# Per-pair order of the projections: all four rotated key products first, the second output-weight product among the queries

## The reference

```
q_lat = x @ Wq_down;  kv_lat = x @ Wkv_down          # x is layer-normalised
q = [q_lat @ Wq_up , rope(q_lat @ Wq_rope)]          # 16 heads, 64 + 64 columns
k = [kv_lat @ Wk_up, rope(x @ Wk_rope)]
out = softmax(causal(q k^T * scale)) @ (kv_lat @ Wv_up)
x = x + out @ Wo
x = x + (silu(h @ up^T) * (h @ gate^T)) @ down^T     # ternary weights, h = layernorm(x)
```

## Time and profile before

| | |
|---|---|
| median of 3 runs | 1917.61 us (1916.95 to 1923.71) |
| profiled execution | 1922.49 us |
| its span | 1920.7 us |
| TensorE busy | 1849.0 us, 96% of the span |
| VectorE, ScalarE, GpSimd busy | 70%, 54%, 27% |
| mean granted TensorE clock | 0.985 of full speed |

### The profile page before, as it was taken

One profiled execution on the slowest core, in us unless ns is written; L12 is line 12 of the kernel. 1 busy time (PEld: TensorE's weight loads), 2 busy tenths in 40 slices (PEclk: granted clock), 3 DMA queues, 4 the chain that ended last, 5 costly groups with the idle time before them and its releaser, 6 DMA issues. The chain is left out here.

```text
span 1920.7 us, 30945 instructions
## 1 busy us (share of the span) xinstructions
PE 1849.0 (96%) x10898; PEld 1611.7 (84%) x10898; DVE 1337.0 (70%) x2818; ACT 1037.2 (54%) x2485; POOL 522.6 (27%) x314
## 2 busy tenths in 40 slices
PE   6899978899999999999999999999999799999998
PEld 4688866889998999999999999999999678777777
DVE  5466646688888888888888888888888633333333
ACT  2223326677777666667676666667666332322232
POOL 4456652111111154234235234234223000000000
PEclk9999988999999999999999999999999889999999
DMA  3399985332231222221221212212110160000000
GB/s 118 118 229 228 219 206 189 91 88 65 79 86 48 66 72 72 62 66 60 57 61 50 78 40 66 68 55 66 39 55 30 37 238 1 22 0 22 4 17 22
DMA packets 96625, 153.31 MB, mean 80 GB/s; under 512 B 12528, under 2 KB 46448, under 8 KB 96240
## 3 DMA queue, kind: packets, MB, share of 16 engines
q1 hardware_dynamic: 84976, 130.66, 23.1%
q10 hardware_dynamic: 11520, 20.98, 4.2%
HBM read 97.06 MB, written 54.53 MB: 79 GB/s over the span
## 5 line engine op out<-in xcount | busy, mean ns | idle before, releaser
L1121 ACT CAST turned_hi<-ps_turn 128x512 fp32r<-128x512 f32 (+1 forms) x576 | 313.6, 571 | 275.4 <-PE ps_turn L1306 271.4
L1077 ACT ACTIVATE probs<-ps_scores,bias 128x512 f32<-128x512 f32 (+3 forms) x640 | 401.9, 641 | 60.0 <-DVE bias L1165 59.7
L1204 DVE TENSOR_TENSOR turned_lo<-ps_turn,turned_hi 128x512 fp32r<-128x512 f32 (+1 forms) x576 | 374.6, 655 | 64.7 <-ACT turned_hi L1121 58.9
L1306 PE MATMUL ps_turn<-ident,probs 128*128 128x128 f32 x2176 | 302.7, 274 | 1.4 <-DVE turned_lo L1204 1.4
L1162 DVE TENSOR_REDUCE negmax<-ps_scores 128x1 f32<-128x512 f32 x384 | 261.9, 686 | 50.5 <-PE ps_scores L1265 45.6
L1306 PEld LDWEIGHTS ps_turn<-ident,probs 128*128 128x128 f32 x2176 | 257.3, 141 | 33.7 <-issue 2.2
L1007 POOL TENSOR_TENSOR q_lo<-q_raw,q_hi 128x512 fp32r<-128x512 f32 x64 | 82.8, 1294 | 687.7 <-ACT q_hi L1069 687.7
L1265 PE MATMUL ps_scores<-k_hi,q_hi 128*128 128x512 f32 (+2 forms) x576 | 233.7, 406 | 7.7 <-ACT probs L1077 7.5
L1325 PE MATMUL ps_o<-turned_hi,kv_hi 128*128 128x256 f32 x1088 | 227.7, 286 | 5.7 <-DVE o_lo L1210 5.7
L1325 PE MATMUL ps_o<-turned_lo,kv_hi 128*128 128x256 f32 x1088 | 224.4, 283 | 0.0
L1325 PE MATMUL ps_o<-turned_hi,kv_lo 128*128 128x256 f32 x1088 | 224.1, 283 | 0.0
(11 more groups left out here) (152 smaller groups left out, 3508.6 us busy)
## 6 DMA issues: line engine op xcount, KB each, us to landing
plainT<-plain_out ACTq DMA_DIRECT2D x64, 256.0 KB, 4.3
rotT<-rot_out SPq DMA_DIRECT2D x64, 256.0 KB, 4.3
all_signs<-signs SPq DMA_DIRECT2D x24, 512.0 KB, 2.8
q_raw<-plainT SPq DMA_DIRECT2D x128, 64.0 KB, 2.4
q_raw<-rotT SPq DMA_DIRECT2D x256, 32.0 KB, 2.1
signs<-in_W_up SPq DMA_DIRECT2D x16, 512.0 KB, 3.6
signs<-in_W_gate SPq DMA_DIRECT2D x16, 512.0 KB, 3.7
signs<-in_W_down SPq DMA_DIRECT2D x16, 512.0 KB, 3.6
```

The lines of the kernel that those rows point to most:

```text
L1077: nc.scalar.activation(probs_of(n, i)[:, h, first_key:first_key + keys], ps_scores[:, pieces.number[args] % RING, 0:keys], ACT.Exp, scale= ...
L1121: nc.scalar.copy(turned[0][:, at, cols(*args)], ps_turn[:, bank, cols(*args)]).then_inc(turned_hi_ready, 1)
L1204: nc.vector.tensor_tensor(turned[1][:, at, cols(*args)], ps_turn[:, bank, cols(*args)], turned[0][:, at, cols(*args)].bitcast(F32), ALU.su ...
L1306: last = nc.tensor.transpose(ps_turn[:, bank, (2 * b + h) * P:(2 * b + h + 1) * P], probs_of(n, i)[:, h, key:key + P], ident[:])
```

## The change

In `usual_order()` the four rotated key products come first, as in `last_order()`; the first head's output-weight product stays behind the second key product, both parts of its weights are split at the head of the pair, the second head's behind the fourth key product. Then come the chunks' rotated queries, plain queries and plain keys. `W_SPLIT` stays behind chunk 1's plain keys, and the second VO product is behind those of chunk 2. In `last_order()` only `VO_LO` moves: it comes directly behind `VO_HI`, ahead of the key product and of the early loads. No instruction is added or taken away.

```diff
@@ usual_order
     for c in range(NC):
-        order += [(VO_HI, c // 2)] * (c % 2 == 0)
-        order += [(ROT, c, 0), (ROT, c, 1)]
-        order += [(VO_LO, c // 2)] * (c % 2 == 0)
-        order += [(PLAIN, c, 0), (PLAIN, c, 1)]
+        order += [(VO_HI, 0), (VO_LO, 0)] * (c == 0)
+        order += [(ROT, c, 0)]
+        order += [(VO, 0)] * (c == 1)
+    order += [(VO_HI, 1), (VO_LO, 1)]
+    for c in range(NC):
+        order += [(ROT, c, 1), (PLAIN, c, 0), (PLAIN, c, 1)]
         order += [(W_SPLIT,)] * (c == 1)
-        order += [(VO, c // 2)] * (c % 2 == 1)
+        order += [(VO, 1)] * (c == 2)
     return order
@@ last_order
     for c in range(NC):
-        order += [(VO_HI, c // 2)] * (c % 2 == 0)
+        order += [(VO_HI, c // 2), (VO_LO, c // 2)] * (c % 2 == 0)
         order += [(ROT, c, 0)]
         order += [(EARLY, 0)] * (c == 0)
-        order += [(VO_LO, c // 2)] * (c % 2 == 0)
         order += [(VO, c // 2)] * (c % 2 == 1)
```

## The result

| | before | changed |
|---|---|---|
| median, 8 runs each | 1918.05 us (1916.95 to 1923.71) | 1913.99 us (1911.35 to 1915.28) |
| ratio, 95% interval | 1 | 0.9972 [0.9960, 0.9983] |
| profiled execution, its span | 1922.49, 1920.7 us | 1913.12, 1911.3 us |
| mean granted TensorE clock | 0.985 | 0.990 |

A second comparison (11 executions of the changed kernel, 19 of the one before) gave 0.9978 [0.9969, 0.9987]. The two together say about 0.9975, that is 4.8 us. The forecast was 6.6 us, a ratio of 0.9966: inside the first interval, 0.0003 outside the second.

A forecast was written before the change was run, and what follows sets the result against it. The prediction took the usual pairs as bound by TensorE's own pace, beside a nearly full memory path. Last pair -7.4 and first pair +0.8 make -6.6 us; 1917.6 - 6.6 = 1911.0 us, range over all 1903 to 1921.

The forecast's parts named there:

- (a) to (d): Usual pairs: rotations, VO splits, `W_SPLIT` and transfers were each checked for a new wait; none expected, change 0.
- (d): Usual pairs, transfers: same bytes, but bunched; plain stores land in 5 to 6 us, cost taken as 0.
- First pair: First pair: the fourth key product waits because the second rotation needs the sine table; cost 0.8 us, bounds 0 and 1.1.
- that stays: First pair: TensorE's present stall of 2.2 us for the first tables remains in either order.
- steps 1 and 2: Last pair: TensorE's stalls of 2.93 and 8.10 us before the two output-weight products both go.
- Step 3: Last pair: matmuls behind each stall run at a clock of 0.50; stalls and slow matmuls make 14.9 us.
- Step 4: Last pair: ScalarE waits for `q_raw`, landing at 283.0 to 283.2, and TensorE for ScalarE; chain moves by 5.4 us.
- Step 5: Last pair: VectorE's splits, rotations and maxima put the first bias at 299.1, 7.8 us earlier; second head gains 7.4 us.
- VectorE is held by GpSimd in the key splits: Rival, last pair: moved splits meet four GpSimd instructions, VectorE's chain ends 2.2 us later; gain 4.4, 1913.2 us; chance 0.15.
- The whole stall goes: Rival, last pair: all 14.9 us of stalls and slow matmuls are gained, less 0.8; 1903.5 us; chance 0.15.
- The burst: Rival, usual pairs: plain stores land later than 7.4 us and TensorE waits, 12.6 us in all; 1923.6 us; chance 0.12.
- The change does not do what it says: Rival, last pair: the second VO product waits as long behind another load or split; 1914 us and up; chance 0.05.

The follow-up runs named there:

- the memset kernel: The changed kernel with only GpSimd's low parts of the queries in stages 1 and 3 replaced by a memset to zero; ratio to before 0.9960 [0.9946, 0.9974].

## Why the prediction was right, step by step

- **Usual pairs, (a) to (d): 0.** Right: no wait, 160.00 of 160.00 us busy. In (d) the landings were forecast at 5 to 6 us and were 3.1 at the median, 5.5 at most: the sign of that effect was wrong, but it lay under TensorE's work either way.
- **First pair: +0.8.** Right in place, before the fourth key product, and in size, 1.0 us by the means of ten profiles. But "that stays", said of the first wait of 2.2 us, was wrong: in the changed kernel it is 0.62 and the new one 2.06, so 0.5 us more in that profile.
- **Last pair, steps 1 and 2: both stalls go.** Right; the products start at 267.29 and 273.41 (forecast: by 266.75 and 272.9, plus the 0.7 us by which this pair began later).
- **Step 3, the slow matmuls.** Right in kind: they come back behind the new wait, seven steps of 0.42 or more from 287.73 to 290.88 where nine were forecast.
- **Step 4, what is late next.** The mechanism is right: ScalarE waits for `q_raw` and TensorE for ScalarE, until 287.73 (forecast 287.0). The landing was forecast at 283.0 to 283.2 and released ScalarE at 284.45. One part of the error is the issue: the first early load left 0.73 us later (269.05 for 268.32), because the pair began 0.68 us later (261.82 for 261.14; 0.3 of that is the execution's) and the load still follows the store of the first key product's sum. The output weight's load, issued at 266.31, was out of SyncE's way. The other part is the 9.7 us taken over from the earlier trace rows: the last query loads took 10.3 to 10.7 us. What made them longer is not shown. Together that is a shift of 4.1 in place of 5.4.
- **Step 5, the splits.** This is the step that failed. "Splits 3.6, rotation 2.4, splits 3.6" took 4.23, 2.4 and 3.52 + 1.28: 1.8 us more, since the moved splits now meet both of GpSimd's query parts and two of its sums. From the first low part to the bias I had 14.7 us; it took 16.1. The first bias was forecast at 299.1 and came at 301.74, the gain there 5.0 in place of 7.8 (5.7 to 6.0 from the start of the last pair). The gain kept to the end was taken as 7.4, from the second head; it too moved by 5.0 (311.89 to 306.93).
- **Rivals.** "VectorE is held by GpSimd in the key splits" was the better forecast: it gave a gain of 4.4 us in all, the runs gave 4.8, and its rows are there. I gave it 0.15, though the earlier trace rows had a split of 1785 ns beside one of 691, and the memset kernel shows its cause. "The whole stall goes" fell as argued: the queries' landing holds ScalarE. The burst did not happen. "The change does not do what it says" did not either: the second VO product waits for nothing.

So the time was met, 1914.0 for 1911.0 (the median before was 0.4 us higher in this comparison), with the path right and two terms too small: the landing by 1.3 us, half of which is the pair's later start, and the splits by 1.4 to 1.8.

## What to carry to other kernels

A stall of 11 us was worth 5, because the engine behind it waited for something else as well; before pricing a stall, find the second arrival (here a landing) and count the gain to it alone. A load issued earlier makes a store on the other queue land later, and delays whoever waits for that store's buffer: look at when each buffer must be free before a load goes in front (here 11.6 us for a store that took 3.3). When splits move on VectorE, lay them beside GpSimd's instructions that read SBUF, and count every meeting (here the key chain was 16.8 us with four and 15.0 with two).

## What the hardware did that I had not expected

- **A small store behind large loads of the other queue.** The same 256 KB store, issued on ScalarE's queue, landed in 3.3 to 3.8 us where it was issued before SyncE's 2 MB or together with the first of them, and in 8.0 to 12.5 us while they were under way. First the changed kernel, then the one with the early loads first:

```profile
wvo<-wvo_out ACTq DMA_DIRECT2D x1, 256.0 KB, 3.3
```

```profile
wvo<-wvo_out ACTq DMA_DIRECT2D x1, 256.0 KB, 12.1
```

  (the earlier trace rows have 9.7.) The prediction weighed a sentence of the Trainium skill, DMA: Bandwidth & Descriptors, "Queues, rings and completion order", on taking turns between queues, by which the store should have landed early; all the profiles with this store behind SyncE's loads speak against that outcome. The same section also says that a transfer's semaphore increment lands only after every earlier write of that DMA engine, across its queues. By that the store's data may have been through early and only its semaphore late; the rows fit it, but none of the runs tells the two apart.
- **The same bytes in less engine time.** With the rotated products first, 226 GB/s took 0.71 of the DMA engines and not 0.92, in the usual order alone as well; a plain store landed in 3.1 us in place of 4.3 at the median. Only the order and the moments of the same transfers differ. What makes it is open. It bought nothing here.
- **The clock at a border.** Between 1514 and 1554 us the granted clock of the same kernel was 0.87 in one execution and 0.74 in another, 4.0 us of span apart. A difference of two single profiles of this kernel is no better than that.
